# Longer loop turns in layers 0 and 2, fronts loaded from two queues, and powers stored in pairs of chunks

## The reference

```python
pw = wins[..., None] ** jnp.arange(DEG_P)
P = jnp.einsum('pbchwi,fcpi->fpbchw', pw, A)
Q = 1.0 + jnp.abs(jnp.einsum('pbchwi,fcpi->fpbchw', pw[..., 1:1 + DEG_Q], Bc))
out = jnp.sum(P / Q, axis=(1, 3))
```

## Time and profile before

| | us |
|---|---|
| median of 3 runs | 9667.91 |
| lowest and highest | 9665.2, 9704.05 |
| the profiled execution | 9659.51 |
| its span, first to last instruction | 9657.6 |

### The profile page before, as it was taken

One profiled execution on the slowest core, in us unless ns is written; L12 is line 12 of the kernel. 1 busy time (PEld: TensorE's weight loads), 2 busy tenths in 40 slices (PEclk: granted clock), 3 DMA queues, 4 the chain that ended last, 5 costly groups with the idle time before them and its releaser, 6 DMA issues. The chain is left out here.

```text
span 9657.6 us, 141494 instructions
## 1 busy us (share of the span) xinstructions
PE 8079.0 (84%) x35042; PEld 2745.1 (28%) x35042; DVE 7784.3 (81%) x9341; ACT 7530.9 (78%) x8315; POOL 6169.8 (64%) x3354
## 2 busy tenths in 40 slices
PE   5999999999999999402998999899899899992799
PEld 2333333333333333100222222222222222220233
DVE  6777777777777776775999999899899999894787
ACT  4666666666666666365999999999999999992887
POOL 3555555555555554002999999999999999992111
PEclk9999999999999999756999999999999999996899
DMA  2000000000000000254333233323332233235555
GB/s 87 12 13 11 12 11 11 11 11 11 13 11 11 12 11 3 110 170 134 70 71 68 59 68 71 69 61 65 71 71 64 60 70 71 65 64 134 132 146 124
DMA packets 258449, 565.42 MB, mean 59 GB/s; under 512 B 71659, under 2 KB 179787, under 8 KB 244183
## 3 DMA queue, kind: packets, MB, share of 16 engines
q1 hardware_dynamic: 221746, 536.51, 22.6%
q0 software_dynamic: 35744, 17.87, 1.0%
HBM read 367.15 MB, written 186.72 MB: 57 GB/s over the span
## 5 line engine op out<-in xcount | busy, mean ns | idle before, releaser
L1226 POOL TENSOR_TENSOR l_a<-l_a 128x1018 f32<-128x1018 f32 x2117 | 3919.7, 1883 | 334.9 <-ACT l_a L1401 327.7
L1356 DVE TENSOR_TENSOR l_r<-l_pps,l_a 128x509 f32<-128x509 f32 x4234 | 2653.6, 680 | 377.7 <-PE l_pps L1239 311.3
L1401 ACT ACTIVATE l_a<-l_a 128x2036 f32<-128x2036 f32 x1194 | 2269.4, 1901 | 52.6 <-ACT l_a L1394 46.8
L1239 PE MATMUL l_qps<-l_mv,wst 123*128 123x509 bf16 x4248 | 1283.8, 384 | 754.8 <-DMA l_mv<-pw 408.3
L1394 ACT ACTIVATE l_a<-l_qps 128x1018 f32<-128x1018 f32 x1593 | 1604.1, 1016 | 172.5 <-PE l_qps L1239 145.8
L599 POOL TENSOR_TENSOR a_pr<-a_pr 128x768 f32<-128x768 f32 x384 | 896.5, 2335 | 807.9 <-DVE a_pr L537 792.0
L1239 PE MATMUL l_pps<-l_mv,wst 123*128 123x509 bf16 x4234 | 1334.8, 381 | 56.5 <-DVE l_r L1356 46.0
L675 ACT ACTIVATE a_g<-a_fps 128x512 f32<-128x512 f32 x1152 | 645.4, 595 | 755.7 <-PE a_fps L419 631.8
L1292 PE MATMUL l_aux<-l_r,l_sums 128*32 128x509 f32 x8448 | 1140.7, 606 | 0.5 <-issue 0.4
L1362 DVE TENSOR_SCALAR l_a<-l_qps 128x1018 int32<-128x1018 int32 x796 | 961.3, 1208 | 9.3 <-PE l_qps L1239 8.0
L537 DVE TENSOR_TENSOR a_pr<-a_qkv,a_at 128x768 f32<-128x768 f32 x576 | 854.8, 1536 | 2.2
(11 more groups left out here) (180 smaller groups left out, 11911.9 us busy)
## 6 DMA issues: line engine op xcount, KB each, us to landing
l_mv<-pw SPq DMA_DIRECT2D x1608, 79.5 KB
l_gx<-g SPq DMA_DIRECT2D x66, 1040.0 KB
l_sh<-planes SPq DMA_DIRECT2D x536, 127.2 KB, 6.2
planes<-l_s SPq DMA_DIRECT2D x66, 1018.0 KB, 4.6
a_xt<-g SPq DMA_DIRECT2D x192, 160.0 KB, 3.3
pw<-pw_hi SPq DMA_DIRECT2D x20, 1000.0 KB
pw<-pw_mid SPq DMA_DIRECT2D x20, 1000.0 KB
pw<-pw_lo SPq DMA_DIRECT2D x20, 1000.0 KB
```

The source lines that it names most:

```text
L1226: g.tensor_tensor(a, a, a, ALU.mult).then_inc(sq_p, 1)
L1239: return t.matmul(out, wst[:, k, n * P:(n + 1) * P], x[:, n // NPP, cols], start=True, stop=True)
L1356: v.tensor_tensor(to, pps[:, (2 * m + h) % P_BANKS, 0:SUB], pair_of(A, m)[:, h, :], ALU.mult).then_inc(mul_done, 1)
L1401: s_.activation(a, a, ACT.Abs_reciprocal_sqrt, bias=1.0).then_inc(root_done, GROUP)
```

## The change

1. Layer 0's loop has 20 rounds in a turn (`ROUNDS`), so 3 turns where there were 15; the ring stays 4 deep.
2. Layer 2's loop has 18 supertiles in a turn, so 3 turns where there were 11, and the last 12 supertiles are straight code. SP's own loop keeps its 6 (`QUEUED`).
3. `norm0` loads its quarters 0 and 2 from SP and 1 and 3 from ACT, and stores in the same way.
4. `layer1` loads `X` in two halves and `G`'s pieces in turn from SP and ACT. The add runs over rows with 16 adjacent columns inside, the statistics are taken of blocks of 32 rows and 16 columns, and each piece's maximum is reduced to one value a row at once.
5. `powers` stores two chunks with one DMA; two slots of two chunks each stand where three of one were.
6. The rows of ones in `mv` come from HBM (`ones`, written in layer 1), and VectorE's memsets of `mv` go. PE waits for them and for `sums` and `pick` in one semaphore, `c_in`.
7. `layer3` loads `X` from SP and `Y` from ACT, into 5 slots; the weights are made at piece 6 and no longer at piece 3; the stores of `g3` are shared by both queues.

The diff, cut to these:

```diff
@@ layer 0's loop
+ROUNDS = 20
...
-    with engine.Fori(0, (LEAD_OUT - LEAD_IN) // TURNS) as thrice:
-        for i in range(TURNS):
-            body(Plan(thrice * TURNS + (LEAD_IN + i), (LEAD_IN + i) % TURNS, LEAD_IN))
+    with engine.Fori(0, (LEAD_OUT - LEAD_IN) // ROUNDS) as again:
+        for i in range(ROUNDS):
+            body(Plan(again * ROUNDS + (LEAD_IN + i), (LEAD_IN + i) % TURNS, LEAD_IN))
@@ norm0
+        def load(e, k):
+            e.dma_start(X[:, k * HW // 4:(k + 1) * HW // 4], x[:, k * HW // 4:(k + 1) * HW // 4]).then_inc(x_in[k], 16)
...
             def _(sp):
-                for k in range(4):
-                    sp.dma_start(X[:, k * HW // 4:(k + 1) * HW // 4], x[:, k * HW // 4:(k + 1) * HW // 4]).then_inc(x_in[k], 16)
+                for k in (0, 2):
+                    load(sp, k)
                 norm.sync_part(sp, pair)
...
             def _(act):
+                for k in (1, 3):
+                    load(act, k)
                 norm.scalar_part(act)
+                for k in range(1, W // COLS, 2):
+                    store(act, k)
@@ layer1
+            def load(e, half):
+
+                rows = slice(half * HW // 2, (half + 1) * HW // 2)
+                e.dma_start(X[:, rows], x[:, rows]).then_inc(x_in[0], 16)
+                for k in range(half, LOADS, 2):
+                    n = HW // LOADS
+                    e.dma_start(G[:, k * n:(k + 1) * n], x1[:, k * n:(k + 1) * n]).then_inc(x_in[k], 16)
...
-                            e.wait_ge(x_in[j], 16)
-                            if j == 0:
-                                e.wait_ge(xb_in, 32)
-                            link(v.scalar_tensor_tensor(image[:, at, :], laid[:, at, :], shift0[:], image[:, at, :], ALU.add, ALU.add))
+                            e.wait_ge(x_in[j], 16 if j else 64)
+                            link(v.scalar_tensor_tensor(image[:, :, at], laid[:, :, at], shift0[:], image[:, :, at], ALU.add, ALU.add))
+                            v.tensor_reduce(tops[:, j, :], image[:, :, at], AX.X, ALU.max)
 
                     def chunk(k, n):
-                        at = k * n // H
-                        return image[:, at:at + n // H, :]
+                        j, part = divmod(k, norm.CHUNKS // LOADS)
+                        rows = n // cols
+                        return image[:, part * rows:(part + 1) * rows, j * cols:(j + 1) * cols]
 
                     norm.vector_part(dve, link, chunk, chunk_in)
                     v.memset(norm2.eps[:], GN_EPS)
-                    link(v.reduce_max(top[:, 0:1], X[:], AX.X))
+                    link(v.reduce_max(top[:, 0:1], tops[:].rearrange("p k h -> p (k h)"), AX.X))
@@ powers
-    BUF = 3
-    CH = 800
+    CH, SLOTS2 = 800, 2
...
+        def piece(t, k, i):
+
+            return t[:, k // 2 % SLOTS2, i, k % 2 * CH:k % 2 * CH + chunks[k][1]]
+
+        def wait_stored(e, q):
+            e.wait_ge(stored[q % SLOTS2], (q // SLOTS2 + 1) * STORES)
...
-                for k, (at, n) in enumerate(chunks):
+                for q in range(NPAIRS):
+                    at, n = chunks[2 * q][0], sum(n for _, n in chunks[2 * q:2 * q + 2])
+                    done = min(2 * q + 2, len(chunks))
                     for m, (t, ready) in enumerate(((hi, hi_ready), (mid, mid_ready), (lo, lo_ready))):
-                        sp.wait_ge(ready, (k + 1) * DEG)
-                        sp.dma_start(lines[m, :, :, :, at:at + n], t[:, k % BUF, :, 0:n]).then_inc(stored[k % BUF], 16)
-                    if k == 1:
+                        sp.wait_ge(ready, done * DEG)
+                        sp.dma_start(lines[m, :, :, :, at:at + n], t[:, q % SLOTS2, :, 0:n]).then_inc(stored[q % SLOTS2], 16)
+                    if q == 0:
...
-                    if k >= BUF:
-                        act.wait_ge(stored[u], k // BUF * STORES)
+                    if k // 2 >= SLOTS2:
+                        wait_stored(act, k // 2 - SLOTS2)
@@ layer2
-BODY = 6
+BODY, QUEUED = 18, 6
...
+    for s in range(LAG_LATE, LAG_LATE + NSUP % BODY * NSUB * NPAIR2):
+        step(NSUP // BODY, s)
...
-                sp.dma_start(sums[:], l2w[0]).then_inc(c_in, 16)
-                sp.dma_start(pick[:], l2w[1]).then_inc(c_in, 16)
...
                 for g in range(SLOTS):
-                    sp.wait_ge(mv_cleared, g + 1)
                     load_supertile(g, g)
+                    sp.dma_start(mv[KROWS - 3:KROWS, g].rearrange("p c n -> p (c n)"), ones).then_inc(c_in, 16)
+                    if g == 0:
+                        sp.dma_start(sums[:], l2w[0]).then_inc(c_in, 16)
+                        sp.dma_start(pick[:], l2w[1]).then_inc(c_in, 16)
...
-                pe.wait_ge(c_in, 32)
+                pe.wait_ge(c_in, 80)
...
-                for u in range(SLOTS):
-                    v.memset(mv[:, u], 1.0).then_inc(mv_cleared, 1)
@@ layer3
+            YSLOTS = 5
...
                     for k in range(PIECES):
                         n = HW // PIECES
                         sp.dma_start(X[:, k * n:(k + 1) * n], x2[:, k * n:(k + 1) * n]).then_inc(x_in[k], 16)
-                        if k >= 3:
-                            sp.wait_ge(added, k - 2)
...
-                        sp.dma_start(Y[:, k % 3, :], rows).then_inc(x_in[k], 16)
...
+                    store(sp, 0)
...
-                        if p == 3:
+                        if p == 6:
...
+                    for k in range(PIECES):
+                        if k >= YSLOTS:
+                            act.wait_ge(added, k - YSLOTS + 1)
...
+                        act.dma_start(Y[:, k % YSLOTS, :], rows).then_inc(x_in[k], 16)
                     norm.scalar_part(act)
+                    store(act, 1)
```

More of the change, by code:

```diff
@@ L207, in _ @@
             def _(sp):
-                for k in range(4):
-                    sp.dma_start(X[:, k * HW // 4:(k + 1) * HW // 4], x[:, k * HW // 4:(k + 1) * HW // 4]).then_inc(x_in[k], 16)
+                for k in (0, 2):
+                    load(sp, k)
                 norm.sync_part(sp, pair)
[L211 to L214, removed]
+                for k in range(0, W // COLS, 2):
+                    store(sp, k)
                 sp.wait_ge(edges, 2)
@@ L717, in _, with layer1 @@
                 steps(act, body)
-def layer1(nc, x, x1, bias0, x2, pair, w1, raw2, pieces, wst, pw):
+def layer1(nc, x, x1, bias0, x2, pair, w1, raw2, pieces, ones, wst, pw):
     TILE = 1024
@@ L784, in _ @@
                     sp.dma_start(rest2[:], raw2).then_inc(raw_in, 16)
[L785 to L789, removed]
-                        sp.dma_start(G[:, k * n:(k + 1) * n], x1[:, k * n:(k + 1) * n]).then_inc(x_in[k], 16)
+                    sp.dma_start(shift0[:], bias0).then_inc(x_in[0], 16)
+                    load(sp, 0)
                     norm.sync_part(sp, pair)
@@ L798, in _ @@
                         sp.dma_start(flat, part2[:, m, :]).then_inc(stored, 16)
+                    sp.wait_ge(one_made, 1)
+                    sp.dma_start(ones.rearrange("r n -> (r n)").rearrange("(p n) -> p n", p=ONES), one[:]).then_inc(stored, 16)
                     for k in range(4):
@@ L922, in _ @@
                     s = nc.scalar
+                    load(act, 1)
                     norm.scalar_part(act)
@@ L951, in powers @@
     STORES = 3 * 16
+    NPAIRS = (len(chunks) + 1) // 2
     with ExitStack() as ctx2:
@@ L969, in powers @@
         wst_in = sem("pw_wst_in")
-        stored = [sem(f"pw_stored{u}") for u in range(BUF)]
+        stored = [sem(f"pw_stored{u}") for u in range(SLOTS2)]
         def power(k, i):
@@ L992, in _ @@
                 sp.wait_ge(wst_in, (len(A_PARTS) + 3) * 16)
-                for u in range(BUF):
-                    sp.wait_ge(stored[u], len(chunks[u::BUF]) * STORES)
+                for q in range(NPAIRS - SLOTS2, NPAIRS):
+                    wait_stored(sp, q)
             @block.vector
@@ L1462, in layer3, with store @@
             zeroed, g_ready, g_stored = sem("l3_zeroed"), sem("l3_g_ready"), sem("l3_g_stored")
+            def store(e, half):
+                for k in range(PIECES):
+                    e.wait_ge(g_ready, k + 1)
+                    lo = k * ROWS // CROWS
+                    hi = lo + ROWS // CROWS if k < PIECES - 1 else NCK
+                    for j in range(half * QUAD // 2, (half + 1) * QUAD // 2):
+                        to = g3[lo:hi, :, :, j, :].rearrange("k e c n -> (e c) k n")
+                        src = G[32 * j:32 * j + 32, lo * CROWS:hi * CROWS, :].rearrange("p (k r) w -> p k (r w)", r=CROWS)
+                        e.dma_start(to, src).then_inc(g_stored, 16)
             with nc.Block() as block:
```

100 lines of the change are left out of this document (47 added, 53 removed).

## The result

The changed kernel took 9571.83 us in the median of 4 runs (9565.68 to 9594.88), the kernel before beside it 9685.95: ratio 0.9886, 95% interval 0.9861 to 0.991. Run again on another occasion it took 9564.83 (ratio 0.9894, 0.9872 to 0.9916).

| stage | before | after | difference | forecast |
|---|---|---|---|---|
| norm0 | 58.3 | 63.0 | +4.8 | +5 |
| layer 0 | 3818.7 | 3767.5 | -51.2 | -50.4 |
| layer 1 | 229.0 | 218.9 | -10.1 | -14.5 |
| powers | 381.5 | 366.2 | -15.3 | -19 |
| layer 2 | 4287.7 | 4264.7 | -23.0 | -50.4 + 18 |

What follows compares the result with a forecast made beforehand. The prediction held layer 2 bound by ScalarE, layer 0 by TensorE and powers by DMA. Its terms summed to -125.9 us from the profiled 9659.5, giving 9533.6, or 9542 as a median; range 9480 to 9592.

Steps and rivals of the forecast that it cites:

- Loops, -100.8: Layers 0 and 2: longer turns leave fewer branches back, saving 50.4 us in each.
- Rival (b): Loops: the pause belongs to a place in the code, so long bodies pay as often; total 9643, chance 0.05.
- norm0, +5: norm0: two queues share the engines, so quarter 0 lands later and the chain behind it shifts by 5 us.
- Layer 1, -14.5: Layer 1's front: pieces -0.9 us, last maximum -16.1, start 2.5 later; bounds -26 and -5.
- Powers, -19: Powers: eight full DMA engines limit the stores; pairs, one every 10.4 us, save 19 us net.
- Rival (a): Powers: descriptors bound the stores, so pairs halve them; total 9432, chance 0.09.
- rival (c): Powers: pair stores go as slowly as the reads' packets, 18.3 us a store; total 9779, chance 0.03.
- Layer 2's start, +18: Layer 2: PE waits for the last row of ones behind all 72 loads, starting 18 us later; bounds +10 and +20.
- Layer 3's first part, -14.6: Layer 3's front: earlier last landing -20.5 us, weights' arithmetic moved +5.9; bounds -37 and -3.
- -20.5 on the last landing: Layer 3's front: five slots and ACT's own queue keep engines full, so the last Y load lands 20.5 us earlier.
- Two queues give 0 to -2: Layer 3's stores of g3, already at 93.3% DMA share: a second queue saves 0 to 2 us.
- rival (d): Layers 1 and 3 give nothing; total 9571, chance 0.13 together with other small misses.

Runs made afterwards that it cites:

- e1: The changed kernel with short loop turns back, 4 rounds in layer 0 and 6 supertiles in layer 2: 9676.54 us, ratio 1.0002 to the kernel before.
- e10: e6 with Y loaded from both queues and single turns of 60 rounds in layer 0 and 66 supertiles in layer 2: 9463.64 us, ratio 0.9774.
- e5: The changed kernel with norm0, layer 1's loads and g3's stores from SP alone, and powers storing single chunks as before: 9608.15 us, ratio 0.9942.
- e6: e4 with norm0 and layer 1 from SP alone, first row of ones, sums and pick ahead of layer 2's loads: 9534.1 us, ratio 0.9871.
- e4: The changed kernel with each powers store and each layer 3 Y load cut into eight DMAs of 16 partitions: 9563.76 us, ratio 0.9895.
- e7: e6 with powers' store packets aligned to 64 B in HBM and Y's images loaded in another order: 9526.84 us in one run.
- e8: e6 with powers' stores and Y's loads split: images 0 to 3 from SP, 4 to 7 from ACT: 9535.58 us, ratio 0.985.
- e9: e8 with powers' stores of images 4 to 7 issued by GpSimd instead of ScalarE: 9459.95 us, ratio 0.9775.
- e3: The changed kernel with all three rows of ones, sums and pick loaded ahead of layer 2's 72 loads: 9549.23 us, ratio 0.9873.
- c0: The changed kernel run again without any edit, for its spread: 9564.83 us, ratio 0.9894 to the kernel before.
- e2: The changed kernel with the tensor of ones placed behind all others in HBM: 9576.93 us, ratio 0.9898.

## Why the prediction was right, and where its sum was not

1. **Loops, -100.8.** Right in kind, place and size: -51.2 in layer 0 and -51.0 from the first `l_cs` to the last, and 53.1 and 53.8 when they were taken back (e1). Rival (b) is out. That long bodies cost nothing held, and more: I had costed the register operations at 0 with a bound, since ScalarE seemed to be the one that mattered in layer 2; in layer 0, where PE does, I hadn't asked. e10 puts up to 26 us there, if it is they.
2. **norm0, +5.** +4.8; back to 58.0 in e5 and 58.3 in e6.
3. **Layer 1, -14.5.** The pieces are right (8.3 us). The add's operands were misread, though: before, `X` and the result were strided and `G` was not; now `G` is, and `X` and the result lie in runs of 16. The 3.7 us held all the same. The term that failed is "the start is 2.5 later": it is 6 to 7 later, and one queue gives it back (e5 28.3, e6 28.6). I had let only two pieces share the rate. The queues of the changed kernel from 3831 to 3845, and from 3845 to 3858 (q1 is SP's, q10 ACT's), show more:

```profile
q10 hardware_dynamic: 212, 4.75, 81.8%
q1 hardware_dynamic: 229, 0.43, 11.5%
...
q1 hardware_dynamic: 186, 4.16, 74.7%
q10 hardware_dynamic: 172, 1.28, 24.6%
```

   SP's first load, `l_rest`, has 128 packets of 3360 B, eight for each engine; an engine takes one of them and then one of ACT's 32768 B (1.2 us), so `l_rest` took 9.6 us where it had taken 2, and `l_shift`, 128 packets of 4 B, came between ACT's in the same way. In 14 us SP's queue moved 0.43 MB, and SP's half of `X` began at 3846.5. ACT's was in at 3844, and ACT went on with pieces that nobody needed yet: some 400 packets of them by 3865, SP 170. Without the whole of `X` no piece can be added. One queue for all undoes it; e5 and e6 didn't try `l_rest` alone elsewhere.
4. **Powers, -19.** -15.3, with the spacing (10.2 us) and share (0.52) foretold. The reason behind it, eight engines full, stands: the 3200 B packets took 133 ns for 130 foretold, with at least eight always under way. What it suggested and I tried in e4, that sixteen engines would go faster, was wrong: with DMAs of 16 partitions something else gives 192 GB/s, it isn't alignment (e7), and only DMAs on both halves of the partitions at once, from two queues, moved more (e8, e9). Rival (a) is out: the spacing didn't halve. Two slips of the working: rival (c)'s 18.3 us a store go with 14 B/ns, so 229 ns a packet and not 291, and the bound of -129 is -122 by its own terms (229.7 against 351.5). The Trainium skill (SBUF — State Buffer, section Door 1: The DMA port swizzle) says that DMA speed goes by how many of SBUF's 16 ports the partitions reach, and that partitions 0 to 63 reach only eight. The traces of e4, e8 and e9 (192, 289 and 228 GB/s) are in keeping with it; that it is the ports and not the second queue was not measured. I had not weighed it.
5. **Layer 2's start, +18.** Right as a mechanism: PE waits for the last row of ones, and goes when these are first (e3). Mis-sized: +28 in the first trace, +24 in c0. The term that was too small is the time of the 72 loads: the 1440 packets were taken at the pace of before, 39 us, and took 47 (c0) to 51, at 309 to 338 ns a packet and not 278. With the ones ahead of everything (e3) it is 308 still, and addresses are out (e2), so why they are slower is open.
6. **Layer 3's first part, -14.6.** Both halves failed and nearly met. "-20.5 on the last landing" gave -0.4 in the first trace and +3 to +10 in c0 and e1 to e3. While X and Y both flow they slow each other: 219 GB/s in c0 (4.82 MB in the 22 us from 8684) at a share of 1.02, with X's 8192 B packets at 636 ns; packets of that size took 311 in layer 1. I had taken each at its own rate and added (86 us for 111, which is 25 less and not the 20.5 written), and blamed the three slots for the rest; with five the last landing came no earlier. "Two queues give 0 to -2" on the stores of `g3` gave -9 in every run that had them. That the two nearly cancel is luck. The Trainium skill (DMA: Bandwidth & Descriptors, section Rules for kernel authors) says that spreading DMAs over queues doesn't help bandwidth. For norm0 that held (+4.8); for packets of 2080 B the trace disagrees (259 against 338 GB/s), and the measurement decides. But here too SP stores partitions 0 to 63 and ACT 64 to 127, as in e8, in DMAs of 32, so the gain may be the halves' and not the second queue's.

Summed by e1, points 2 to 6 are 0.0% (interval -0.08 to +0.12), not -25 us. The forecast of -126 against -114 and -107 measured was carried by the loops alone: the rest was off by 25 us, which the range could bear. Nearest to it was rival (d).

## What to carry to other kernels

A loop's price is in its trace before anything is changed: take the interval of something that happens once an iteration, inside a turn and across one. A DMA share near a round fraction names how many engines are busy, not what they would meet if there were more: sixteen with DMAs of 16 partitions moved 192 GB/s and eight with DMAs of 128 moved 197, so try it before counting on it. And where one operand is needed whole before anything can start, a second queue that fetches what comes later takes rate from it.

## What the runs showed of the hardware, unlooked for

- Of the engines in these loops only PE pays for a taken branch, 3.3 to 5.3 us; DVE, ACT and POOL 45 to 72 ns (e1). A turn costs the stage 4.2 to 4.4 us in layer 0 and 6.3 to 6.7 in layer 2.
- Where two queues share the engines they take turns by packet, not by bytes: eight packets of 3360 B an engine took 9.6 us beside packets of 32768 B at 1.2 us, and 2 us alone.
- Two queues of 2080 B packets, one on partitions 0 to 63 and one on 64 to 127, moved 338 GB/s where one queue on all moved 259.
- Stores from 16 partitions at a time moved 192 GB/s on 16 engines from one queue; from two queues, one on each half of the partitions, 289.
- VectorE, 2048 elements in float32: an add took 4.69 us with one input and the result strided by 128 elements, 3.70 with one input strided by 128 and the other and the result in runs of 16; another add instruction took 2.29 with all contiguous; four BN_STATS over 512 elements took 3.75 strided by 128, 2.46 in runs of 16.
- The same code of layer 3's second part varied by 48 us between executions, 0.5% of the whole.
